# The cross-attention's projections of batches 2 to 7 as float32r products of rows cut in two

## What is computed

```python
q = jnp.einsum('oc,bct->bot', Wq, target) + bq[None, :, None]
k = jnp.einsum('oc,bcs->bos', Wk, source) + bk[None, :, None]
v = jnp.einsum('oc,bcs->bos', Wv, source) + bv[None, :, None]
...
dot = jnp.einsum('bhdt,bhds->bhts', q, k) / math.sqrt(HEAD_DIM)
dot = mask * dot - (1.0 - mask) * NEG
amap = jax.nn.softmax(dot, axis=-1) * mask
out = jnp.einsum('bhts,bhds->bhdt', amap, v)
...
x = _layernorm(x + _L0_xattn_ref(x, ctx_2048, ...), axis=-1)
```

## Time and profile before

| | us |
|---|---|
| median of 3 runs | 1651.98 |
| lowest and highest | 1651.69 and 1657.13 |
| the profiled execution | 1652.93 |
| its span on the core | 1650.7 |
| PE busy in the span | 1470.6 (89%) |
| POOL busy in the span | 806.6 (49%) |

### The profile page before, as it was taken

How to read it: one execution, slowest core, us unless ns; L and a number is a source line. 1 busy time by engine, 2 the same in 40 slices (tenths; PEclk the granted TensorE clock), 3 DMA queues, 4 the chain that set the end, 5 groups by cost and what they waited for, 6 DMA issues and landing times. The chain is left out here.

```text
span 1650.7 us, 28337 instructions
## 1 busy us (share of the span) xinstructions
PE 1470.6 (89%) x7422; PEld 1027.6 (62%) x7423; DVE 950.9 (58%) x1379; ACT 710.3 (43%) x1328; POOL 806.6 (49%) x650
## 2 busy tenths in 40 slices
PE   6988989889999999998256999999999999999990
PEld 5767767634444444442145878778787878877770
DVE  2333242677787778784294555555555555555555
ACT  4212121157777777777123234434434434444220
POOL 4424242443456545644333466666666576486322
PEclk9999999989999999999577999999999999999995
DMA  6101003264665475541362455565556565373326
GB/s 214 49 26 47 13 13 56 47 102 67 108 118 106 80 130 103 86 83 40 101 249 71 103 149 143 154 152 143 155 141 159 133 177 152 98 192 79 58 57 211
DMA packets 93712, 180.13 MB, mean 109 GB/s; under 512 B 17576, under 2 KB 20392, under 8 KB 93000
## 3 DMA queue, kind: packets, MB, share of 16 engines
q1 hardware_dynamic: 73944, 133.88, 31.8%
q0 software_dynamic: 18544, 44.84, 13.6%
q10 hardware_dynamic: 1152, 0.52, 0.2%
HBM read 115.55 MB, written 33.49 MB: 90 GB/s over the span
## 5 line engine op out<-in xcount | busy, mean ns | idle before, releaser
L824 DVE TENSOR_REDUCE stage<-ps_a 128x2 f32<-128x1024 f32 x256 | 300.5, 1218 | 87.9 <-PE ps_a L1045 87.3
L1600 POOL TENSOR_TENSOR we_split<-we_raw,we_split 128x512 f32 (+1 forms) x192 | 250.5, 1543 | 98.7 <-ACT we_split L1591 97.0
L638 ACT ACTIVATE probs<-ps_b 128x512 f32<-128x512 f32 x512 | 277.9, 595 | 43.6 <-PE ps_b L1060 41.3
L1885 PE MATMUL ps_y<-we_split,hT 128*128 x912 | 234.2, 406 | 4.0 <-DVE hT L1816 3.3
L1885 PE MATMUL ps_g<-we_split,xT 128*128 x912 | 230.6, 402 | 5.1 <-issue 4.2
L1885 PE MATMUL ps_u<-we_split,xT 128*128 x912 | 231.9, 403 | 0.0
L1885 PEld LDWEIGHTS ps_g<-we_split,xT 128*128 128x128 f32 x912 | 171.8, 190 | 53.1 <-issue 13.0
L1885 PEld LDWEIGHTS ps_y<-we_split,hT 128*128 128x128 f32 x912 | 167.8, 190 | 41.7 <-issue 6.3
L1885 PEld LDWEIGHTS ps_u<-we_split,xT 128*128 128x128 f32 x912 | 166.7, 189 | 35.0
L1701 POOL DMA_INDIRECT scratch_acc<-x_keep,to_rows x76 | 121.2, 1594 | 110.6 <-issue 50.8
L1751 ACT ACTIVATE hT<-ps_h 128x512 fp32r<-128x512 f32 x76 | 45.3, 596 | 296.0 <-PE ps_h L1866 296.0
(11 more groups left out here) (214 smaller groups left out, 2114.6 us busy)
## 6 DMA issues: line engine op xcount, KB each, us to landing
we_raw<-in_w_expert SPq DMA_DIRECT2D x192, 256.0 KB, 3.0
stack<-xT_raw SPq DMA_DIRECT2D x192, 128.0 KB, 5.4
we_bias<-in_b_expert SPq DMA_DIRECT2D x16, 768.0 KB, 4.0
stage<-in_w SPq DMA_DIRECT2D x5, 1024.0 KB, 4.8
xT_raw<-in_xT SPq DMA_DIRECT2D x4, 1024.0 KB, 6.3
x_tok<-in_x POOLq DMA_DIRECT2D x16, 256.0 KB, 3.0
late<-o_pair SPq DMA_DIRECT2D x128, 32.0 KB
late<-scratch_inv SPq DMA_DIRECT2D x16, 256.0 KB
```

Of the source, the lines that this page charges most:

```text
L638: nc.scalar.activation(probs[:, n % 3, h], src[:], ACT.Exp, scale=DH ** -0.5).then_inc(b_kept, 1)
L824: nc.vector.tensor_reduce(out[:, :, i, k % NC], ps_a[i][:], AX.X, ALU.max, negate=True).then_inc(a_kept[i], 1)
L1600: nc.gpsimd.tensor_tensor(lo, W["raw"][:, k, c], hi, ALU.subtract).then_inc(W["lo"], 1)
L1885: mm = nc.tensor.matmul(out[:], left[:, a, c], w[:, bass.ds(par, 1), k, b, c].squeeze(1), start=(n == 0), stop=(n == len(passes) - 1))
```

## The change

For batches 2 to 7 the operands of the projections are cut into an upper float32r part (hi) and the remainder (lo), and each projection is made in three passes, hi by hi, lo of the one by hi of the other, and the reverse, with float32r products; lo by lo is left out. Batches 0 and 1 stay as they were. GpSimd makes the cuts: the weights w_qk and w_v once, x of a batch in one piece (128x1024), the context in two halves (128x2x256 each, positions 0 to 255 and 256 to 511). A cut is a copy and a subtraction. From batch 2 on all contexts are loaded into the one buffer in stage, and the two buffers of old are used for the parts. The parts lie in memory that the first attention has done with; the inverses move from y_sb to kv_mask.

The order of GpSimd's list changes as the third and fourth pieces of the diff say: x's cut stands ahead of fill_v(b + 1, 0), the first context cut ahead of finish_heads(b - 1), and fill_v(b + 1, 1) and the second context cut behind it. TensorE waits for cut_step: for x in step 12, for the context's first half in step 14 and for its second half in step 15. The core of the diff (the allocations are left out):

```diff
@@ -160,7 +172,8 @@
         v_stage = k_sb[:].rearrange("p a (b c) -> p a b c", b=2)
         ctx_in = [V["ctx"], v_sb[:]]
         mask_in = [V["mask"]] + [u_sb[:, i] for i in range(3)]
-        o_all, inv = o_pair, y_sb[:, 0:H * T // P]
+        o_all, inv = o_pair, kv_mask[:, 0:H * T // P]
+        x_cut, ctx_cut, w_qk_cut = (x_hi, x_lo), (ctx_hi, ctx_lo), (w_qk_hi, w_qk_lo)
 
         ps_a = [ctx.enter_context(nc.psum_tensor(f"ps_a{i}", [P, 2, T], F32)) for i in range(2)]
         ps_b = [ctx.enter_context(nc.psum_tensor(f"ps_b{i}", [P, T], F32)) for i in range(RING)]
@@ -253,6 +267,12 @@
 
         USE, EARLY = uses_of_ring()
 
+
+        cuts = [("w_qk",), ("x", 2), ("ctx", 2, 0), ("ctx", 2, 1), ("w_v",)]
+        for b in range(3, B):
+            cuts += [("x", b), ("ctx", b, 0), ("ctx", b, 1)]
+        CUT = {piece: 2 * (i + 1) for i, piece in enumerate(cuts)}
+
         def ring_bank(at):
             return ps_b[at % 2] if at < EARLY else ps_b[(at - EARLY) % RING]
 
@@ -264,9 +284,11 @@
         @block.sync
         def _(sp):
             def load_ctx(b):
-                if b >= 2:
-                    sp.wait_ge(b_made, USE["v", b - 2, NC - 1] + 1)
-                sp.dma_start(ctx_in[b % 2], A["ctx"][b]).then_inc(ctx_loaded[b % 2], 16)
+                if b == 2:
+                    sp.wait_ge(b_made, USE["v", 0, NC - 1] + 1)
+                elif b > 2:
+                    sp.wait_ge(cut_step, CUT["ctx", b - 1, 1])
+                sp.dma_start(ctx_in[b % 2 if b < 2 else 0], A["ctx"][b]).then_inc(ctx_loaded[b % 2 if b < 2 else 0], 16)
 
             def load_mask(b):
                 if b >= 4:
@@ -464,6 +486,29 @@
                                             v_stage[:, i, j].rearrange("p (h d) -> p h d", h=H),
                                             mask_col[:, b, c:c + 1], None, ALU.mult).then_inc(v_filled, 1)
 
+            def cut(piece, whole, hi, lo):
+                nc.gpsimd.tensor_copy(hi, whole).then_inc(cut_step, 1)
+                pool.wait_ge(cut_step, CUT[piece] - 1)
+                nc.gpsimd.tensor_tensor(lo, whole, hi.bitcast(F32), ALU.subtract).then_inc(cut_step, 1)
+
+            def cut_x(b):
+                if b > 2:
+                    pool.wait_ge(b_made, USE["qk", b - 1, 2, 1] + 1)
+                cut(("x", b), x[:, 2 * b:2 * b + 2, :], x_hi, x_lo)
+
+            def cut_ctx(b, h):
+                pool.wait_ge(ctx_loaded[0], 16 * (b - 1))
+                pool.wait_ge(b_made, USE["v", b - 1, 2 * h + 1 if b > 2 else NC - 1] + 1)
+                cols = slice(h * C, (h + 1) * C)
+                cut(("ctx", b, h), ctx_in[0][:, :, cols], ctx_hi[:, :, cols], ctx_lo[:, :, cols])
+
+            def cut_w_qk():
+                pool.wait_ge(y_added, NT)
+                pool.wait_ge(y_stats, 3 * NT)
+                pool.wait_ge(w_turned, 8)
+                pool.wait_ge(b_made, USE["qk", 1, 3, 1] + 1)
+                cut(("w_qk",), w_qk[:], w_qk_hi, w_qk_lo)
+
             def finish_heads(b):
                 pool.wait_ge(inv_loaded, 32 * b + 32)
                 for i in range(2):
@@ -580,13 +625,25 @@
                 if b + 1 < B:
                     split(b + 1, 2)
                     split(b + 1, 3)
+                    if b == 0:
+                        cut_w_qk()
+                    if b + 2 < B:
+                        cut_x(b + 2)
                     fill_v(b + 1, 0)
-                    fill_v(b + 1, 1)
+                    if 0 < b and b + 2 < B:
+                        cut_ctx(b + 2, 0)
                 if b >= 1:
                     finish_heads(b - 1)
+                if b + 1 < B:
+                    fill_v(b + 1, 1)
                 if b + 2 < B:
+                    if b == 0:
+                        cut_ctx(b + 2, 0)
+                    cut_ctx(b + 2, 1)
                     split(b + 2, 0)
                     split(b + 2, 1)
+                if b == 0:
+                    cut(("w_v",), w2[:, 2], w_v[:, 0], w_v[:, 1])
             normalize(B - 2)
             finish_heads(B - 1)
             normalize(B - 1)
@@ -1011,22 +1068,41 @@
 
             def project_qk(b, i, h):
                 qk, o = i % 2, i // 2
-                if qk and b > 0 and o == 0 and h == 0:
-                    pe.wait_ge(ctx_loaded[b % 2], 16 * (b // 2 + b % 2))
-                if not qk and o == 0 and h == 0:
+                if qk and b == 1 and o == 0 and h == 0:
+                    pe.wait_ge(ctx_loaded[1], 16)
+                if not qk and b < 2 and o == 0 and h == 0:
                     pe.wait_ge(y_stats, 3 * (2 * b + 2))
+                if b >= 2 and o == 0 and not qk and h == 0:
+                    pe.wait_ge(cut_step, CUT["x", b])
+                if b >= 2 and o == 0 and qk:
+                    pe.wait_ge(cut_step, CUT["ctx", b, h])
                 out = bank("qk", b, i, h)
                 cols = slice(h * C, (h + 1) * C)
-                for c in range(2):
-                    rhs = ctx_in[b % 2][:, c, cols] if qk else x[:, 2 * b + c, cols]
-                    mm = nc.tensor.matmul(out[:, 0:C], w_qk[:, qk, c, o], rhs, start=(c == 0), stop=(c == 1))
+                if b < 2:
+                    for c in range(2):
+                        rhs = ctx_in[b % 2][:, c, cols] if qk else x[:, 2 * b + c, cols]
+                        mm = nc.tensor.matmul(out[:, 0:C], w_qk[:, qk, c, o], rhs, start=(c == 0), stop=(c == 1))
+                else:
+                    passes = [(c, wi, xi) for wi, xi in SPLITS for c in range(2)]
+                    for n, (c, wi, xi) in enumerate(passes):
+                        rhs = (ctx_cut if qk else x_cut)[xi][:, c, cols]
+                        mm = nc.tensor.matmul(out[:, 0:C], w_qk_cut[wi][:, qk, c, o], rhs, start=(n == 0), stop=(n == 5))
                 mm.then_inc(b_made, 1)
 
             def project_v(b, sc):
+                if b == 2 and sc == 0:
+                    pe.wait_ge(cut_step, CUT["w_v",])
                 out = bank("v", b, sc)
-                for c in range(2):
-                    mm = nc.tensor.matmul(out[:, 0:C], ctx_in[b % 2][:, c, sc * P:(sc + 1) * P],
-                                          w2[:, 2, c, :], start=(c == 0), stop=(c == 1))
+                rows = slice(sc * P, (sc + 1) * P)
+                if b < 2:
+                    for c in range(2):
+                        mm = nc.tensor.matmul(out[:, 0:C], ctx_in[b % 2][:, c, rows], w2[:, 2, c, :],
+                                              start=(c == 0), stop=(c == 1))
+                else:
+                    passes = [(c, wi, xi) for wi, xi in SPLITS for c in range(2)]
+                    for n, (c, wi, xi) in enumerate(passes):
+                        mm = nc.tensor.matmul(out[:, 0:C], ctx_cut[xi][:, c, rows], w_v[:, wi, c], start=(n == 0),
+                                              stop=(n == 5))
                 mm.then_inc(b_made, 1)
 
             def scores_max(k, i):
```

More of the change, by code:

```diff
@@ L114, in lent, with lent_at @@
             return nc.alloc_sbuf_tensor_at(name, shape, F32, offset=nc.sbuf_base - size)[:]
+        def lent_at(name, shape, offset):
+            return nc.alloc_sbuf_tensor_at(name, shape, F32R, offset=offset)[:]
+        w_qk_hi = lent_at("w_qk_hi", [P, 2, 2, 2, P], nc.sbuf_base - 4 * math.prod(stage.shape[1:]))
         w_raw = stage[:].rearrange("p (i c d) -> p i c d", i=2, c=KC)
@@ L128, in attention @@
         x_tok = sb("x_tok", [P, 2, D])
+        x_hi = lent_at("x_hi", [P, 2, D], nc.sbuf_base - 8 * D)
         k_sb = sb("k_sb", [P, 2, D])
         v_sb = sb("v_sb", [P, 2, D])
+        ctx_lo = lent_at("ctx_lo", [P, 2, D], nc.sbuf_base - 8 * D)
         u_sb = sb("u_sb", [P, TPG, D])
+        y_sb = sb("y_sb", [P, D])
+        w_v = lent_at("w_v", [P, 2, 2, C], nc.sbuf_base - 8 * D)
         kv_mask = sb("kv_mask", [P, P])
         kv_sb = sb("kv_sb", [P, KC, P])
+        o_sb = sb("o_sb", [P, D])
+        ctx_hi = lent_at("ctx_hi", [P, 2, D], nc.sbuf_base - 8 * D)
         o_pair = sb("o_pair", [P, 2, D])
@@ L137, in attention @@
         o_rn = sb("o_rn", [P, H])
-        o_sb = sb("o_sb", [P, D])
         oT_split = sb("oT_split", [P, 2, KC, P], F32R)
-        y_sb = sb("y_sb", [P, D])
+        x_lo = lent_at("x_lo", [P, 2, D], nc.sbuf_base - 8 * D)
         stats = sb("stats", [P, 6])
@@ L150, in attention @@
         w_qk = sb("w_qk", [P, 2, 2, 2, P])
+        w_qk_lo = lent_at("w_qk_lo", [P, 2, 2, 2, P], nc.sbuf_base - 8 * D)
         full = sb("full", [P, 2, T])
@@ L204, in attention @@
         first_step, first_lo = sem("first_step"), sem("first_lo")
+        cut_step = sem("cut_step")
         qk_masked, qk_hi, qk_lo = sem("qk_masked"), sem("qk_hi"), sem("qk_lo")
```

## The result

| | before | after |
|---|---|---|
| median of the runs | 1652.89 us (4 runs, 1651.69 to 1657.13) | 1711.91 us (4 runs, 1705.93 to 1713.03) |
| profiled execution | 1652.93 us, clock 0.951 | 1705.93 us, clock 0.934 |
| the cross-attention stage, from the first scores of batch 0 to the start of the last step of batch 7 | 436.0 us | 491.2 us |

The kernel after takes 1.0345 times as long, with a 95% interval of 1.0314 to 1.0376. The forecast was 1702 us, with a range of 1686 to 1722. The profiled execution is the shortest of the four after, 6 us under their median; before, it is at the median. Outside the stage the profiled executions differ by 2.2 us in favour of the kernel after (53.0 in all, 55.2 in the stage).

What follows compares the result with a forecast made beforehand. TensorE was taken to set the pace of the cross-attention stage. 1652.9 us, plus 41.9 for waits on GpSimd's late cut net of projection savings, plus 7 for the lowered clock, gave 1702, range 1686 to 1722.

Steps and rivals of the forecast that it cites:

- the path of the wait: Step 15, batches 1 to 5: TensorE waits some 10 us for the second context cut, queued behind finish_heads and fill_v.
- (a): Rival: the wait for the second context cut is hidden and only the projections' saving remains, 1642 us; chance 0.08.
- (b): Rival: the inverses' DMA lands sooner, so the wait shrinks to 4 us and the total is 1668; chance 0.07.
- The tail, 13.6 us: From finish_heads' start to the next batch: finish_heads 7.39, fill_v 3.22, cut 1.96, semaphores 0.1, projection 0.91 us.
- Part 4: TensorE's clock falls to half after each of five waits: 11 us in all, +7 net, ends 0 and +14.
- The upper end, 14: Highest clock cost after the waits, +14 us, if the logits' 16-column products keep the clock low for longer.
- 43.7 for the waits: Time added to batches 1 to 5 together by TensorE's wait for the second context cut, +43.7 us.
- less 1.8: Gain from shorter projections in batches 0 and 6: 0.6 and 1.2 us.
- part 3: GpSimd's order: the second context cut comes late and TensorE waits for it in batches 1 to 5; sum +41.9 us.
- part 1: Projections as six float32r instructions at 0.118 us: 0.91 us instead of 1.06, saving 0.15 in each of 72.
- (c): Rival: float32r passes don't overlap weight load and stream, 0.225 us each, total 1729; chance 0.08.
- The cuts at nothing: GpSimd's added cuts, 7.8 us per batch, fit its idle time and cost nothing; uncovered, up to 5.9 per batch.

Runs made afterwards that it cites:

- e4: The kernel after with fill_v(b + 1, 1) back ahead of finish_heads, the second context cut still behind it; 1695.55 us, 1.0272 of before.
- e7: The kernel after with 2.5 us more GpSimd multiplications in five batches, behind the wait for the inverses and ahead of the context cut; 1724.38 us, 1.0439 of before.
- e3: The kernel after with 40 unused float32r products on TensorE ahead of the wait for the second context cut, batches 1 to 5; 1699.92 us, 1.0291 of before.
- e1: The kernel after with fill_v(b + 1, 1) and the second context cut moved ahead of finish_heads(b - 1) on GpSimd; 1645.14 us, 0.9969 of before.
- e8: The kernel of e1 with the cut of x moved, from batch 1 on, behind the first context cut; 1637.09 us, 0.9917 of before.
- e6: The kernel after with 2.5 us more GpSimd multiplications in each of batches 2 to 6, ahead of the wait for the inverses; 1716.7 us, 1.0403 of before.
- e5: The kernel before with only fill_v(b + 1, 1) moved behind finish_heads(b - 1) on GpSimd, no cuts or new products; 1651.28 us, 1.0009 of before.

## Why the prediction came out as it did

**What bounds the kernel, and the path of the wait: right.** The forecast said five stretches of about 10 us, each ended by the subtraction into ctx_lo. They are 9.30, 9.99, 10.18, 10.91 and 11.06 us. finish_heads still waits for the inverses' DMA, and longer than in the earlier trace rows, since the second fill_v no longer stands ahead of it. Rivals (a), a hidden wait, and (b), inverses that land sooner, are refuted by this: finish_heads starts 49.97, 51.07, 54.37, 55.02 and 54.39 us into batches 1 to 5.

**The tail, 13.6 us: a little short.** From finish_heads to the next batch it was 663.74 - 649.68 = 14.06 us in batch 4, and 14.07 to 14.10 in the others. GpSimd's part, 12.4 us, is near the 12.6 worked out. The difference is TensorE's projection, 1.57 us and not 0.91, because it runs at half clock right behind the wait. Part 4 had left this out. That the tail is paid one for one, e4 and e7 show, with 3.15 us less and 2.55 more of it in each batch.

**The clock: the term that was mis-sized.** It was taken in part 4 as 11 us gross and 7 net. The steps 0 to 3 of batches 2 to 6 lost 1.5, 3.2, 3.2, 2.4 and 2.35 us against the same steps at the upper clock (12.6), and each projection behind a wait lost 0.66 (3.3): 15.9 gross. The kernel before paid 1.3, 2.0 and 1.3 us of this kind in its batches 5, 6 and 7, which leaves 11 net; part 4 had not counted its batch 7. The windows of after around the end of batch 3 show the two parts of one such loss, with a return to 1.00 between them:

```profile
587.70:598.00 10.30, 4.92 (x20) 2.49 (x22) 0.32 (x1) 1.56 (x3) 9.91 (x11) 0.50 0.00 0
598.00:601.40 3.40, 3.40 (x32) 2.30 (x28) 2.36 (x2) 1.74 (x4) 1.46 (x2) 1.00 0.02 5
601.40:608.20 6.80, 6.80 (x31) 2.29 (x24) 4.29 (x8) 4.31 (x10) 0.38 (x1) 0.50 0.16 42
```

The earlier trace rows had only the second of them for a model. Steps 1 and 2, which the earlier trace rows have at 6.49 us in batch 4 and at 8.94 in batch 6, where the clock was low, took 609.10 - 600.35 = 8.75 in batch 4 here, as forecast. What was missed is step 0, 5.69 us in place of 4.22, and the projection ahead of it. The second stretch may have other causes than the idle time, since e3 has it where little idle is left and e1 where there is none. The upper end, 14, was tied to the logits' narrow products, and whether they play a part no run shows.

**The sum.** In the stage: 43.7 for the waits, less 1.8, plus 11 make 52.9 against 55.2 measured. The rest, 2.3, lies between the start of step 8 and finish_heads, a stretch that part 3 took to be left alone by the change. It took 24.29, 23.38, 23.33, 24.08 and 24.23 us in batches 1 to 5, and before 23.43, 23.21, 23.13, 23.43 and 22.50: 3.6 more in all, less some 1.3 of small terms, such as the steps, each 0.02 shorter than worked out. What made the inverses later no run shows. With 2.2 us saved outside the stage, the profiled execution is 1705.93 against the forecast's 1701.8. The median is 6 us higher still; the three other executions have a mean clock of 0.929 to 0.931 against 0.934, and where they lost the time isn't known.

**The projections: right.** 0.90 against the forecast's 0.91, and a step with one takes 3.22 where it took 3.39. The six instructions of the projection of 614.64 start at 614.64, 614.87, 614.99, 615.10, 615.21 and 615.33, so the last four distances are 0.115 each, near the 0.118 that the weight loads of the earlier trace rows gave; going in and out takes 0.2 more, as in part 1. Rival (c), 0.225 each, is refuted. By the columns alone, 0.107, the projection would take 0.84. The figure of the Trainium skill cited in part 1 (0.109, a projection of 0.85) is under what was measured by 0.05. e8 shows the whole gain of 10.8 us and 3 more: 72 times 0.02, since a step is 0.17 shorter and not 0.15, and 1.3 in batch 7, which takes 44.85 us in it to the start of its last step and 46.16 before, where the clock fell.

**The cuts at nothing: wrong by some microseconds.** The cover was there for GpSimd's own time, but not for VectorE's. In the kernel after this is worth 2.6 us in batch 1, much of it hidden by the wait that follows; in e1 it and the clock behind it take 2.3 us of the projections' gain in batch 1, and in e6 it stands ahead of the 4.5 us that steps 9 and 10 of batch 2 lost. The Trainium skill (SBUF — State Buffer, SBUF: two separate sides) has an exclusive lock between the two engines, held for a whole instruction, which on VectorE's side concerns instructions with two inputs in SBUF and those in a two-port mode. The rows of 425.5 us agree: VectorE's two small instructions end with GpSimd's. I had read VectorE's busy time as all that mattered of it.

## What to carry to other kernels

- On an engine that works in order, put what another engine needs now ahead of anything that waits for a DMA. Here one call on the wrong side of such a wait was worth 62 to 67 us (e1), and every instruction behind the wait was paid in full (e4, e7), while the order without an urgent instruction behind it showed no cost (e5).
- Price an idle time of TensorE at its length and at the half clock that follows it, from the first product behind the wait on.
- Work given to an idle GpSimd is not free if VectorE has short instructions between SBUF tiles at that time: look at what they would hold, and place the long ones beside VectorE's reads of PSUM.

## What the runs showed of the hardware

- VectorE's copy of 128x16 from SBUF to SBUF took 1.61 us beside a GpSimd subtraction of 128x1024 (after; 2.36 in e6), and 0.51 beside none of that length (e8); its 128x16 subtraction 1.21 against 0.17. In e8 two of VectorE's maxima from PSUM took 2.36 us from 428.50 beside GpSimd's cut of x (428.32 to 431.83), the same as without it.
- TensorE's granted clock fell to 0.50 with 2.0 us of idle left and 9.4 us of dense products ahead of it (e3, start of batch 4), and with 1.42 left behind batch 2, while it stayed at 1.00 behind batch 4 with 1.56 left. It was also at 0.50 from 511 to 517 us of e1, with TensorE busy throughout and in the 6 us ahead. What decides between them, these runs don't tell.
- A float32r product of 256 columns with its own 128x128 weight load costs 0.115 us from start to start in a row of six at the upper clock (after, 614.87 to 615.33), and one of 512 columns 0.23 in a row of forty (e3); an exact product's instruction 0.22.
